# Attention block on one core: projection jobs in pieces of one step each, value accumulation in one piece in the steps that carry a job, statistics of x in the other half batch

## What is computed

```python
def attn(x, Wq, Wk, Wv, Wo):                 # 16 query heads of 16, 4 key/value heads
    q, k, v = x @ Wq, x @ Wk, x @ Wv
    k, v = repeat(k, 4), repeat(v, 4)        # each key/value head serves 4 query heads
    q, k = rope(q), rope(k)
    p = softmax(q @ k.T / sqrt(256))
    return concat_heads(p @ v) @ Wo
def ffn(x, weight, alpha, bias):
    w = ternary(weight) * alpha              # -1, 0, 1 by a threshold of 0.7 mean |weight|
    return x @ w.T + bias
x = x + layernorm(attn(layernorm(x)))
x = x + layernorm(ffn(layernorm(x)))
```

## Time and profile before

| | |
|---|---|
| profiled execution | 1706.93 us, span 1705.0 us |
| granted TensorE clock, mean | 0.953 |
| PE busy | 1494.1 us (88%) |
| VectorE (DVE) busy | 1389.6 us (81%) |
| ScalarE (ACT) busy | 1230.1 us (72%) |
| POOL busy | 642.6 us (38%) |
| the chain that ended last | PE 46%, DVE 31%, issue 12%, DMA 4% |

### The profile page before, as it was taken

How to read it: one execution, slowest core, us unless ns; L and a number is a source line. 1 busy time by engine, 2 the same in 40 slices (tenths; PEclk the granted TensorE clock), 3 DMA queues, 4 the chain that set the end, 5 groups by cost and what they waited for, 6 DMA issues and landing times.

```text
span 1705.0 us, 41144 instructions
## 1 busy us (share of the span) xinstructions
PE 1494.1 (88%) x13810; PEld 521.7 (31%) x13810; DVE 1389.6 (81%) x1899; ACT 1230.1 (72%) x2357; POOL 642.6 (38%) x703
## 2 busy tenths in 40 slices
PE   4589998989989899998999989998999998889872
PEld 3123233333333233332333323332333322222222
DVE  3697899878998789978898879977899789999914
ACT  1067888767877678777787768776788778878770
POOL 2121442454334443344425544254434354323230
PEclk8579999999999899999999999998999999999996
DMA  2311311113120320213111131202202121111010
GB/s 93 89 42 28 93 37 57 27 41 87 43 63 12 93 58 19 64 29 103 32 49 39 40 87 43 60 14 86 63 22 62 28 77 36 49 33 34 20 42 16
DMA packets 72805, 85.65 MB, mean 50 GB/s; under 512 B 17552, under 2 KB 58384, under 8 KB 71056
## 3 DMA queue, kind: packets, MB, share of 16 engines
q1 hardware_dynamic: 72592, 82.86, 17.3%
HBM read 46.66 MB, written 24.64 MB: 42 GB/s over the span
## 4 chain that ended last, share of the span: by engine, by line
PE 46%; DVE 31%; issue 12%; DMA 4%; POOL 3%; ACT 3%; SPq 1%; DVEq 0%; ACTq 0%; POOLq 0%
DVE row_max L1033 23%; PE pv L848 15%; PE smax L826 14%; PE ring L929 4%; PE ring L910 3%; PE ring L937 3%; PE ring L870 2%; DMA sums<-heads 2%; PE ring L916 2%; ACT heads L777 2%; DMA out<-res 1%; DVE sy_bn L1016 1%; ACT probs L734 1%; POOL res L442 1%; DVE sf_bn L1016 1%
## 5 line engine op out<-in xcount | busy, mean ns | idle before, releaser
L1033 DVE TENSOR_REDUCE row_max<-smax 128x1 f32<-128x1024 f32 x1024 | 1196.5, 1213 | 205.1 <-PE smax L826 203.9
L734 ACT ACTIVATE probs<-ring 128x512 f32<-128x512 f32 x2048 | 1098.8, 597 | 177.8 <-PE ring L870 159.5
L826 PE MATMUL smax<-k_rows,q_rows 48*128 48x512 f16 x2048 | 638.4, 393 | 107.5 <-DVE row_max L1033 89.8
L848 PE MATMUL pv<-probs,v_cols 128*32 128x256 f32 x8192 | 667.1, 398 | 33.4 <-ACT heads L777 33.0
L870 PE MATMUL ring<-q_rows,k_rows 50*128 50x512 f16 x2048 | 637.7, 389 | 0.1
L826 PEld LDWEIGHTS smax<-k_rows,q_rows 48*128 48x128 f16 x2048 | 128.8, 94 | 552.3 <-DVE row_max L1033 399.8
L848 PEld LDWEIGHTS pv<-probs,v_cols 128*32 128x32 f32 x8192 | 163.4, 108 | 429.4 <-issue 305.7
L870 PEld LDWEIGHTS ring<-q_rows,k_rows 50*128 50x128 f16 x2048 | 148.5, 94 | 37.3 <-ACT probs L734 15.7
L453 POOL TENSOR_TENSOR attnT<-pairs,inv_rows 128x512 f32<-128x512 f32 x31 | 39.5, 1273 | 276.0 <-DMA inv_rows<-inv_sums_dram 246.1
L436 POOL TENSOR_TENSOR act<-act,bias_sb 128x256 f32<-128x256 f32 x60 | 42.4, 728 | 118.6 <-ACT act L768 118.6
L721 ACT ACTIVATE rot_in<-ring 128x512 f32<-128x512 f32 x40 | 23.9, 597 | 83.8 <-PE ring L910 71.3
(11 more groups left out here) (130 smaller groups left out, 1024.2 us busy)
## 6 DMA issues: line engine op xcount, KB each, us to landing
q_stage_dram<-q_parts SPq DMA_DIRECT2D x48, 256.0 KB, 2.5
q_rows<-q_stage_dram SPq DMA_DIRECT2D x32, 384.0 KB, 5.6
x_in<-in_L_attn_x SPq DMA_DIRECT2D x8, 1024.0 KB, 5.9
pairs<-heads SPq DMA_DIRECT2D x64, 128.0 KB
inv_rows<-inv_sums_dram SPq DMA_DIRECT2D x32, 256.0 KB
res<-in_L_attn_x SPq DMA_DIRECT2D x16, 512.0 KB, 4.5
out<-res SPq DMA_DIRECT2D x16, 512.0 KB, 3.1
k_rows<-k_stage_dram SPq DMA_DIRECT2D x64, 96.0 KB, 3.3
```

What stands on the lines that cost most here:

```text
L734: eng.activation(probs[:, s % PSLOTS, j, :], ring[:, n % RING, :], ACT.Exp, scale=score_unit).then_inc(ring_read, 1)
L826: mm = eng.matmul(smax[:, side, c, :], q_rows[at:to, qc, kv * KVP + jp, qt * P:(qt + 1) * P], k_rows[at:to, kv, c * 512:(c + 1) * 512], st ...
L848: mm = eng.matmul(pv[j * VCOLS:(j + 1) * VCOLS, cols], v_cols[:, g, kt, :], probs[:, s % PSLOTS, j, cols], start=(kt == 0 and part == 0), ...
L1033: eng.tensor_reduce(row_max[:, g % 2, at:at + 1], smax[:, side, :, :].rearrange("p c n -> p (c n)"), AX.X, ALU.max).then_inc(max_read, 1)
```

## The change

Each job takes one step and is at most half as large as before: Q and K are cut into 256-column pieces, V into four pieces of two row tiles, WO and FF into one row tile each. XT has a step for each of its four. V moves from step 20 of the qc = 0 half into steps 0 to 3 of the qc = 1 half that follows; XT moves to steps 0 to 3 of the qc = 0 half; the statistics and the normalisation of x move from there to the qc = 1 half ahead of it (steps 8 to 14 and 15). In a step with a job (other than MT) the values are added in one piece of 512 columns behind the second pair. The tables of POOL's and SP's positions move too: the rotation of both Q halves to step 22, ahead of the bias at 26, and that of K to 18.

```diff
-PRO = {11: [("XT", 0, 0), ("XT", 1, 0)], 12: [("XT", 0, 1), ("XT", 1, 1)],
-       13: [("K",)], 17: [("Q", 0, 0)], 18: [("Q", 0, 1)], 20: [("V",)]}
-
-PRO1 = {5: [("Q", 1, 0)], 6: [("Q", 1, 1)]}
-PRO1_LEAD = {4 - LEAD: [("Q", 1, 0)], 5 - LEAD: [("Q", 1, 1)]}
-
-EPI = {8: [("WO", 0)], 9: [("WO", 1)],
-       19: [("HT", 0), ("HT", 1)], 24: [("FF", 0)], 25: [("FF", 1)]}
...
-X_MOM, A_MOM = (0, 1, 2, 5, 6, 7, 8, 8), (9, 9, 10, 10)
-Y_MOM, F_MOM = (13, 14, 15, 16), (28, 28, 29, 30)
+PRO_FIRST = {11: [("XT", 0, 0), ("XT", 1, 0)], 12: [("XT", 0, 1), ("XT", 1, 1)], 14: [("K", 0)], 15: [("K", 1)],
+             17: [("Q", 0, 0, 0)], 18: [("Q", 0, 0, 1)], 19: [("Q", 0, 1, 0)], 20: [("Q", 0, 1, 1)]}
+PRO = {0: [("XT", 0, 0)], 1: [("XT", 1, 0)], 2: [("XT", 0, 1)], 3: [("XT", 1, 1)],
+       4: [("Q", 0, 0, 0)], 6: [("Q", 0, 0, 1)], 7: [("Q", 0, 1, 0)], 12: [("Q", 0, 1, 1)],
+       14: [("K", 0)], 15: [("K", 1)]}
+
+PRO1 = {0: [("V", 0)], 1: [("V", 1)], 2: [("V", 2)], 3: [("V", 3)],
+        12: [("Q", 1, 0, 0)], 14: [("Q", 1, 0, 1)], 15: [("Q", 1, 1, 0)], 16: [("Q", 1, 1, 1)]}
+PRO1_LEAD = {2 - LEAD: [("V", 0)], 3 - LEAD: [("V", 1)], 4 - LEAD: [("V", 2), ("V", 3)],
+             6 - LEAD: [("Q", 1, 0, 0)], 7 - LEAD: [("Q", 1, 0, 1)],
+             8 - LEAD: [("Q", 1, 1, 0)], 9 - LEAD: [("Q", 1, 1, 1)]}
+
+EPI = {8: [("WO", 0)], 9: [("WO", 1)], 10: [("WO", 2)], 11: [("WO", 3)],
+       19: [("HT", 0), ("HT", 1)],
+       24: [("FF", 0)], 25: [("FF", 1)], 26: [("FF", 2)], 27: [("FF", 3)]}
...
+X_MOM_FIRST, X_MOM = (0, 1, 2, 5, 6, 7, 8, 8), (8, 9, 10, 11, 12, 12, 14, 14)
+A_MOM, Y_MOM, F_MOM = (9, 10, 11, 12), (15, 15, 16, 16), (29, 29, 30, 30)
...
-X_NORM, A_NORM, Y_NORM, ACT_SPLIT, BIAS, F_NORM = 9, 11, 17, 20, 26, 31
-K_ROT, Q_ROT, Q1_ROT = 15, 27, 7
...
-K_SWAP = 14
-K_STAGE = 22
-Q0_STAGE, Q1_STAGE, Q_LOAD = 30, 14, 6
+X_NORM_FIRST, X_NORM, A_NORM, Y_NORM, ACT_SPLIT, BIAS, F_NORM = 9, 15, 13, 17, 20, 26, 31
+K_ROT, Q_ROT, Q1_ROT = 18, 22, 22
+K_SWAP = 17
+K_STAGE = 23
+Q0_STAGE, Q1_STAGE, Q_LOAD = 30, 30, 6
+ALL = (0, 2)
...
+    def values_at(self, s):
+
+        return {1: ALL} if any(job[0] != "MT" for job in self.jobs(s)) else {1: (0, 1), 3: (1, 2)}
...
-                        if i % 2 and ((h.scores and s >= LAG) or (h.flush and s < LAG)):
-                            values(h, s - LAG, i // 2)
+                        if i in parts:
+                            values(h, s - LAG, *parts[i])
...
                         elif kind == "Q":
+                            at = a[0] * HALF + a[2] * HALF // 2
                             for dt in range(DT):
-                                mm = eng.matmul(dst, wq_sb[:, dt, a[1], :, :, :].rearrange("p i r h -> p (i r h)"),
-                                                xT[:, dt, a[0] * HALF:(a[0] + 1) * HALF],
-                                                start=(dt == 0), stop=(dt == DT - 1))
+                                mm = eng.matmul(dst[:, 0:HALF // 2],
+                                                wq_sb[:, dt, a[1], :, :, :].rearrange("p i r h -> p (i r h)"),
+                                                xT[:, dt, at:at + HALF // 2], start=(dt == 0), stop=(dt == DT - 1))
                         elif kind == "V":
-                            for t in range(KT):
+                            for t in range(2):
                                 for dt in range(DT):
+                                    at = (2 * a[0] + t) * P
                                     mm = eng.matmul(dst[:, t * HKV * HD:(t + 1) * HKV * HD],
-                                                    xT[:, dt, t * P:(t + 1) * P], wv_sb[:, dt, :],
+                                                    xT[:, dt, at:at + P], wv_sb[:, dt, :],
                                                     start=(dt == 0), stop=(dt == DT - 1))
...
```

More of the change, by code:

```diff
@@ L113, in __init__ @@
     def __init__(self, b, qc, scores=True, maxima=STEPS, turned=range(1, HKV + 1), pro=None, pro1=None,
[L114 removed]
+                 epi=None, base=0, first=0, steps=STEPS, load_x=None, mom=None, flush=True,
                  after=()):
@@ L126, in __init__ @@
         self.load_x = load_x
+        self.mom = mom if mom is not None else load_x if scores else None
+        self.early = pro is not None and mom is not None
+        self.x_mom = X_MOM_FIRST if self.early else X_MOM
+        self.x_norm = X_NORM_FIRST if self.early else X_NORM
         self.flush = flush
@@ L151, in jobs @@
         if self.pro is not None:
-            out += PRO.get(s, [])
+            out += (PRO_FIRST if self.early else PRO).get(s, [])
         if self.pro1 is not None:
@@ L298, in schedule @@
         def schedule(half, eng, prepare=None):
-            h = Half(0, 0, scores=False, maxima=0, turned=(), pro=0, flush=False)
+            h = Half(0, 0, scores=False, maxima=0, turned=(), pro=0, mom=0, flush=False)
             half(h)
@@ L456, in roots @@
         def roots(eng, h, s):
-            if h.pro is not None and s == X_NORM:
-                root(eng, st_x, KT, x_mom, x_norm, h.pro)
+            if h.mom is not None and s == h.x_norm:
+                root(eng, st_x, KT, x_mom, x_norm, h.mom)
             if h.epi is not None:
@@ L476, in between @@
                     split_k(eng, h.pro)
-                if s == (Q_ROT0 if h.alone else Q_ROT):
+                if s == Q_ROT:
                     rotate_q(eng, h, h.pro, 0)
                     split_q(eng, h.pro, 0)
-            if h.pro1 is not None and s == (Q1_ROT if h.scores else 6 - LEAD):
+            if h.pro1 is not None and s == (Q1_ROT if h.scores else 10 - LEAD):
                 rotate_q(eng, h, h.pro1, 1)
@@ L687, in half @@
                         take_v(h, h.b + 1, g)
-                    if h.alone and h.pro is not None and s == K_ROT:
-                        eng.wait_ge(ring_read, h.done("V"))
+                    if h.pro1 is not None and not h.scores and s == 6 - LEAD:
+                        eng.wait_ge(ring_read, h.done("V", 3))
                         for g in range(HKV):
@@ L830, in maxima, with values @@
                     mm.then_inc(max_full, 1)
-            def values(h, s, part):
+            def values(h, s, first, last):
                 step = h.group0 * KT + s
                 g, kt = s // KT % HKV, s % KT
-                if part == 0:
+                if first == 0:
                     if kt == 0:
@@ L845, in values @@
                         eng.wait_ge(ring_read, h.base)
[L846 removed]
+                cols = slice(first * HALF // 2, last * HALF // 2)
                 for j in range(G):
                     mm = eng.matmul(pv[j * VCOLS:(j + 1) * VCOLS, cols], v_cols[:, g, kt, :],
[L849 to L852 removed]
+                                    probs[:, s % PSLOTS, j, cols], start=(kt == 0 and first == 0),
+                                    stop=(kt == KT - 1), skip_group_check=True)
+                if last == 2:
                     mm.then_inc(pv_step, 1)
@@ L859, in half @@
                     mg, mkt = (s + LEAD) // KT, (s + LEAD) % KT
+                    parts = h.values_at(s) if (h.scores and s >= LAG) or (h.flush and s < LAG) else {}
                     for i, j in enumerate(JORDER):
```

77 lines of the change are left out of this document (35 added, 42 removed).

## The result

The changed kernel takes 1683.12 us (median of 4 runs, 1679.8 to 1686.89) against 1708.01 us for the kernel before on the same chip: ratio 0.987, 95% interval 0.985 to 0.990. That is 25 us less, where the forecast said 61 less. The time lies inside the range (1605 to 1689), near its upper end, but the gain is 0.4 of the one forecast. The profiled execution has a span of 1684.8 us, 20.2 less than before; it is the slowest of the four (1686.89 us), 3.8 above their median.

What follows compares the result with a forecast made beforehand. It took neither PE nor DVE to bound throughout; each waits for the other's bursts. Waits 10.0 less and splits 1.4 more gave 8.6 us a round, 52 over six; with 9 outside, 1707 became 1646 us, range 1605 to 1689.

Steps and rivals of the forecast that it cites:

- round's end: End of each loop round: wait at the branch plus PE's lower clock, some 4.7 us before and 5.7 after.
- the slower rival: POOL reaches the bias late behind Q's rotation, DVE stands in step 29; 1730 us at 8 us late; chance 0.06.
- Its own signs of being wrong: DVE waiting for POOL at F's statistics, a job step over 3.2 us, or the lower clock outside the round's end.
- heads: In steps 2, 10 and 26 values wait for ScalarE's heads copy: 0.5 us in five of six steps, 2.5 a round.
- the sum of waits that are left: DVE's waits for PE in a round, summed step by step: 17.2 us against 27.2, so 10.0 less.
- Q, K, WO steps; V; FF; XT; HT: PE's time per job step: 3.07 us for Q, K, WO, 3.04 V, 2.81 FF, 2.63 XT, 3.15 HT.
- the lead between jobs: PE gains on DVE between jobs: 0.48 us for each of seven job groups, 4.2 us off a round's waits.
- the splits: DVE's splits of the maxima beside POOL's work cost 3.7 us a round instead of 2.3, 1.4 more.
- Outside the loop: Gains in the half batches and the rest around the six rounds, less V in the lead: 9 us in sum.
- POOL's work lands on DVE's splits: Full-cost coincidences in the splits idle PE and lower its clock: 9 us a round instead of 3.7, 1681; chance 0.14.
- Pieces do not fill the gaps: Values stay at 1.14 us or job pieces exceed half, no lead regained: 43 us back, 1689; chance 0.12.
- The waits only move: PE is the bound throughout, so only the values' 0.09 x 27 a round is gained: 1691; chance 0.08.

Runs made afterwards that it cites:

- e10: The changed kernel with a loop of three rounds of four half batches in place of six of two; 1670.8 us, 0.981.
- e11: The kernel before with a loop of three rounds of four half batches in place of six of two; 1698.3 us, 0.996.
- e1: The changed kernel with the values in two halves in every step, as before, instead of whole in job steps; 1693.7 us, 0.994.
- e7: The kernel before with values in one piece in job steps and the heads read ahead of the job's copy there; 1668.8 us, 0.977.
- e4: The changed kernel with ScalarE's copy of the heads ahead of its copy of the job's result; 1664.5 us, 0.977.
- e12: The kernel before with only ScalarE's copy of the heads moved ahead of its copy of the job's result; 1675.4 us, 0.982.
- e5: The changed kernel with V in steps 4 to 7 of the qc = 1 half and the heads read early; 1655.0 us, 0.969.
- e8: e5 with values in halves beside XT, HT and FF, except ahead of a copy of the heads; 1663.8 us, 0.975.
- e6: e4 with the store and spread of the inverse sums put behind the row maxima's DMA on SP; 1706.5 us, 1.000.
- after: The changed kernel itself, without further edits; 1683.12 us, 0.987 of the kernel before.
- e9: e5 with a loop of three rounds of four half batches in place of six of two; 1646.8 us, 0.967.

## Why the prediction was right in sign and too large

**Right.** PE's jobs no longer stand in bursts. The segments that lost one are 4.6, 4.2, 2.1, 1.1 and 0.8 us shorter (qc = 1, 3 to 11; qc = 0, 19 to 27, 11 to 19 and 3 to 11; qc = 1, 19 to 27; means of six rounds); those that took work in are 4.1, 2.8 and 2.4 us longer (qc = 1, 11 to 19 and 27 to 3; the round's end). The bias behind the rotation never made F's statistics wait in the loop, so the slower rival had no part in it. The splits of steps 19 (qc = 0) and 27 coincide with POOL.

**Its own signs of being wrong.** Two of three came, and one thing it had ruled out. Job steps in which the values wait for the heads take 3.4 to 3.9 us, over the 3.2 named. The lower clock appears outside the round's end. And DVE waits over 1 us there in three to five places of a round, up to 1.41, where it was to be none.

**The step that failed is the sum of waits that are left.** Over the six rounds DVE's waits for PE fell from 26.6 us a round to 20.9, 5.8 less, where the prediction went from the 27.2 of its one round to 17.2, 10.0 less. Of the 4.2 that are missing 0.6 are its choice of round. The other 3.7 lie in the terms of the sum:

| term, us in a round | forecast | measured |
|---|---|---|
| heads | 2.5, five waits of 0.5 | 3.3, six of 0.32 to 0.81 |
| Q, K, WO steps; V; FF; XT; HT | 3.07; 3.04; 2.81; 2.63; 3.15 | 3.13; 3.11; 2.89; 2.89; 3.23 |
| maxima's DMA in step 8 | none | 0.85 to 1.50 in five rounds, 1.0 on average |
| lower clock outside the round's end | none | 6 us in three rounds, 1.0 on average |
| round's end | 5.7, and 1 more than before | 5.7, and 1.9 more than before (e10, e11) |

The steps are off by a piece's fixed 0.1 us, which whole values at 1.00 half make good, and in XT by the ring: 4 x 0.26 for XT, 8 x 0.08 for FF, 14 x 0.06 for those of Q, K, WO and V where PE sets the pace, 2 x 0.08 for HT, 2.7 us. With 0.8 for the heads, 1.0 for the maxima and 1.0 for the clock these are 5.5 us, 1.8 more than the 3.7; where that was gained these rows don't show. The 4.2 us that the prediction took off for the lead between jobs can't be measured by themselves: without that term its sum is 21.4, half a microsecond from the measured 20.9. So it is shown that the sum was too small, and which waits it lacked, but not how much of its lead is real.

**Terms that it put at nothing.** The prediction let the reductions' busy time stand as it was; it rose by 1.9 us a round (14.9 in all, and e1 ties it to the whole values). Idle time under 0.15 us ahead of a reduction, which no list of waits counts, rose from 0.2 to 1.1 us a round. And the splits cost less, not more. DVE's two groups for them took 21.6 + 16.8 = 38.4 us before and 17.9 + 17.7 = 35.6 now, where 6 x 1.4 more were forecast: before, too, they coincided in more places than the one that the earlier trace rows shows. The round's balance is then closed: waits -5.8, short idle times +1.0, DVE's other idle time -0.4, busy time of the reductions, splits and statistics together +1.6, which gives the 3.5 us by which it became shorter.

**Outside the loop** 9 us were forecast and 1 was lost. The lead and the start of `Half(0, 0)` cost 4.9 us, near the 5.5 put on V there, but the rest of that half gained 1.3 instead of 5.9. `Half(6, 1)` gained 3.4, as forecast, and what follows it lost 0.8 instead of gaining 4.9.

**Of the rivals**, "POOL's work lands on DVE's splits" is closest with its 1681, by luck: the splits cost less than before. One part of it came true, a lower clock outside the round's end, but at 1 us a round and not behind a split. "Pieces do not fill the gaps" (1689) is half right: a job piece takes more than half a job (1.07, 1.04 and 0.76 where 0.96, 0.93 and 0.70 stood), but whole values took 1.00 and not 1.14. "The waits only move" is nearer to the cause. e7 and e4 differ by 4 us, e12 and e7 by 7, so with the heads aside the change is worth 11 us by the medians (8 by the ratios), and about 20 with V out of the slow stretch (e5 against e12).

**What the prediction overlooked** was in its own profile. It read DVE's waits for PE and took them for the cost of the jobs. It did not ask in how many of them PE itself was waiting; the heads were 33.0 us of that, 4.5 in a round, and it priced them only for the changed kernel. The whole-job steps of before were so charged for a wait that has nothing to do with their length, and cutting them left three quarters of it standing (24.3 of 33.0).

What stays open: why the lower clock lasts longest at the round's end with halves (e1), what stops PE a second time there in e8, and why the branches left in e11 cost more than those of before.

## What to carry to other kernels

When engine A waits for B, list B's own waits first: what B waits for is often cheaper to remove than B's work is to move, and here one reordered copy (e12, 30 us) beat a rewritten schedule (25 us). Cutting work into pieces removes nothing, it pays only where a piece lands under time the other engine needs anyway; price each piece with its fixed part, and count the waits as well as their sum. Before a transfer is moved past another on a queue, follow the other one's chain to its last reader (e6).

## What the runs showed of the hardware

- A loop branch costs 4 to 6 us here (24.9 against 30.6, 24.1 against 27.9, 21.6 against 25.7), of which DVE's first wait at it shows 1.3 to 3.4. PE stands idle at it for 3.0 to 4.7 us in after, and around it PE runs at its lower level, granted 0.50, for 3 to 10 us, in e1 for 17 to 31. Half as many branches gave 7 to 12 us (e9 to e11).
- Small VectorE instructions beside a POOL operation took up to 1.16 us instead of 0.17, and reductions of 128x1024 at most 1.226 instead of a median of 1.218. The Trainium skill (SBUF — State Buffer, Who interferes with whom) has it that the two engines block each other for a whole instruction where both use their shared pair of ports, and that a reduction never contends; the trace agrees with both.
- Two reductions in a row start 1.14 us apart and one alone takes 1.23. A change that breaks their runs apart shows as busy time, 14.9 us of it here, and not as waiting.
